# Start rows kept in registers, a region of rows per expert, a shorter plan and three smaller edits in a routed attention and expert kernel

## What is computed

```python
x = x + xattn(layernorm(x), ctx, ctx, mask, Wq, Wk, Wv, bq, bk, bv)   # relu(relu(q k^T)/sqrt(d) + mask) v), relu
h = layernorm(x)
topv, topi = top_k(h @ gate_w, 2);  w = softmax(topv)                  # 8 experts, 2 per token
Y[e] = (silu(h @ Wu[e]) * (h @ Wv[e])) @ Wo[e]
x = x + w[0] * Y[topi[0]] + w[1] * Y[topi[1]]
```

## Time and profile before

| | |
|---|---|
| median of 3 runs | 445.58 us (444.45 to 448.17) |
| profiled execution | 448.33 us, its span 446.6 us |
| busy: TensorE, its weight loads | 92%, 81% |
| busy: VectorE, ScalarE, GpSimd | 78%, 60%, 44% |
| mean granted TensorE clock | 0.982 |
| DMA moved | 97.99 MB, mean 219 GB/s |

### The profile page before, as it was taken

The page is one execution under the profiler, slowest core; times in us unless marked ns, Lnnn a source line. Parts: engine busy times, 40 slices in busy tenths (PEclk is TensorE's granted clock), DMA queues, the critical chain, the costliest instruction groups (busy, mean ns, idle before and its releaser), DMA issues.

```text
span 446.6 us, 10603 instructions
## 1 busy us (share of the span) xinstructions
PE 409.9 (92%) x3066; PEld 362.5 (81%) x3066; DVE 347.0 (78%) x1138; ACT 267.2 (60%) x581; POOL 195.3 (44%) x234
## 2 busy tenths in 40 slices
PE   8999999999999999989898999899999968979790
PEld 6688998888888998878787888799998857968670
DVE  2679899999999999998678888578877656657560
ACT  1677777787877778767575566576664423333230
POOL 2011245555555656653467432333331535554441
PEclk9999999999999999999999999999999999898995
DMA  8713234766666664535768699799746989898831
GB/s 294 236 61 96 94 115 173 280 237 221 236 240 240 239 231 167 181 133 176 262 199 274 234 288 295 238 316 288 228 102 185 322 271 296 273 299 284 280 143 47
DMA packets 53623, 97.99 MB, mean 219 GB/s; under 512 B 8384, under 2 KB 19136, under 8 KB 53440
## 3 DMA queue, kind: packets, MB, share of 16 engines
q1 hardware_dynamic: 41648, 63.21, 45.9%
q0 software_dynamic: 11920, 34.10, 20.2%
HBM read 54.15 MB, written 50.80 MB: 235 GB/s over the span
## 4 chain that ended last, share of the span: by engine, by line
PE 39%; DVE 22%; SPq 16%; issue 9%; ACT 6%; DMA 4%; POOL 1%; POOLq 0%; DVEq 0%; ACTq 0%
PE psQ L1513 6%; SPq L506 6%; PE psQ L1514 6%; PE psQ L1515 6%; DVE st L1122 4%; DVE x L1111 3%; PE psT L1509 3%; PE psS L1513 2%; DVE qpT L932 2%; SPq L521 2%; SPq L528 2%; DMA vp<-acc_dram 2%; PE psS L1515 2%; PE psS L1514 2%; SPq L535 1%
## 5 line engine op out<-in xcount | busy, mean ns | idle before, releaser
L932 DVE TENSOR_TENSOR qT<-psT,qT 128x512 fp32r<-128x512 f32 x103 | 69.3, 686 | 25.1 <-ACT qT L728 24.8
L1513 PE MATMUL psQ<-wuv,qT 128*128 x284 | 87.0, 306 | 0.0
L634 POOL DMA_INDIRECT z_dram<-zb x64 | 71.4, 1116 | 31.3 <-issue 15.2
L1514 PE MATMUL psQ<-wuv,qT 128*128 x284 | 81.1, 286 | 0.0
L1515 PE MATMUL psQ<-wuv,qT 128*128 x284 | 80.7, 284 | 0.0
L1513 PE MATMUL psQ<-qT,wq 128*128 128x256 f32 x256 | 75.2, 294 | 0.0
L1515 PE MATMUL psQ<-qT,wq 128*128 128x256 f32 x256 | 72.4, 283 | 0.0
L1514 PE MATMUL psQ<-qT,wq 128*128 128x256 f32 x256 | 72.4, 283 | 0.0
L728 ACT ACTIVATE qT<-psT 128x512 fp32r<-128x512 f32 x103 | 59.4, 594 | 17.4 <-PE psT L1509 17.4
L1513 PEld LDWEIGHTS psQ<-wuv,qT 128*128 128x128 f32 x284 | 54.2, 191 | 3.2 <-issue 0.2
L1515 PEld LDWEIGHTS psQ<-wuv,qT 128*128 128x128 f32 x284 | 54.7, 192 | 0.0
(11 more groups left out here) (333 smaller groups left out, 1074.2 us busy)
## 6 DMA issues: line engine op xcount, KB each, us to landing
wq<-z_dram SPq DMA_DIRECT2D x42, 264.0 KB, 3.7
xin<-in_x_dram SPq DMA_DIRECT2D x11, 512.0 KB, 3.7
z_dram<-spare SPq DMA_DIRECT2D x17, 264.0 KB, 3.8
qpT<-z_dram SPq DMA_DIRECT2D x17, 264.0 KB, 4.0
acc_dram<-spare SPq DMA_DIRECT2D x17, 256.0 KB, 3.9
xin<-acc_dram SPq DMA_DIRECT2D x16, 256.0 KB, 3.7
vp<-acc_dram SPq DMA_DIRECT2D x14, 256.0 KB, 3.8
kpT<-z_dram SPq DMA_DIRECT2D x10, 264.0 KB, 3.4
```

The source lines that it names most:

```text
L634: pool.indirect_dma_start(out=z_dram, out_offset=bass.IndirectOffsetOnAxis(ap=z_of(b)[:, t, ROW_COL + k:ROW_COL + k + 1].bitcast(U32), axi ...
L932: nc.vector.tensor_tensor(o, a, b, ALU.subtract).then_inc(s, 1)
L1513: pe.matmul(o, w[LO], a[HI], start=first, stop=False)
L1514: pe.matmul(o, w[HI], a[LO], start=False, stop=False)
```

## The change

- **Slots in registers.** SyncE reads the row of a tile from 39 on once, in `load_z`, and keeps it in a register for `load_acc`. The rows of the 14 held tiles are read two at a time ahead of tiles 43 to 49 (`know_held`). Before tile 50 five `load_acc` are issued instead of nine, and later ones follow the `z_dram` loads by four to six tiles instead of two; `load_held` stands behind `load_z` and `load_acc` of its tile instead of ahead.
- **Five places** for what is added to held tiles instead of three.
- **One region of 8192 rows per expert**: firsts from its bottom up, seconds from its top down (a sign is multiplied in where the place is written). The constant rows behind the seconds have fixed addresses and are stored in blocks 4 to 11; `fill_pad` (8 DMAs with a row read, tiles 17 to 24) is gone. `copy_tail` reads two rows instead of one.
- **A shorter plan.** The expert of a tile is its row shifted right by 13 bits. The chains have 10, 15 and 30 instructions instead of 13, 17 and 38, and are cut into tiles in another way; the third part is read out one tile later.
- **Scores wait by chunk**: each chunk waits for its own low half.
- **Logit strips turned plainly**: two 128x128 transposes, and VectorE adds the four strips (`folded`) ahead of the choice of experts.
- **x normalised on ScalarE**: both halves; VectorE's `norm_x` goes from the block.

```diff
 
-CAP = TOK + 2 * P
-DUMMY = K * E * CAP
-NROWS = DUMMY + P
+
+
+LOG_CAP = 13
+CAP = 1 << LOG_CAP
+TOP = TOK + 2 * P
+NROWS = E * CAP
+DUMMY = NROWS - P
...
-PLANNED = (13, 30, 68)
+CONSTS = 20
+
+PLANNED = (10, 25, 55)
 
 
 def ge(eng, sem, value):
...
-        extra = [vp_flat[:, i * D:(i + 1) * D] for i in range(3)]
+        extra = [vp_flat[:, i * D:(i + 1) * D] for i in range(4)] + [kpT_flat[:, 2 * ROW:2 * ROW + D]]
...
                 if 4 <= b.n < 4 + E:
-                    e = b.n - 4
-                    sp.dma_start(z_dram[K * e * CAP:K * e * CAP + P, :], spare[:, :]).then_inc(head_stored, 16)
-                    sp.dma_start(acc_dram[(K * e + 1) * CAP:(K * e + 1) * CAP + P, :], spare[:, 0:D]).then_inc(head_stored, 16)
+                    at = (b.n - 4) * CAP
+                    sp.dma_start(z_dram[at:at + P, :], spare[:, :]).then_inc(head_stored, 16)
+                    sp.dma_start(z_dram[at + TOP:at + TOP + P, :], spare[:, :]).then_inc(pad_stored, 16)
+                    sp.dma_start(acc_dram[at + TOP:at + TOP + P, :], spare[:, 0:D]).then_inc(acc_pad_stored, 16)
 
...
-                row = row_of(t)
-                sp.dma_start(zg_of(t), z_dram[bass.ds(row, P)]).then_inc(z_loaded[q], 16)
-
-            def load_acc(t, row):
+                rows[t] = row_of(t)
+                sp.dma_start(zg_of(t), z_dram[bass.ds(rows[t], P)]).then_inc(z_loaded[q], 16)
+                if t < FIRST_B:
+                    del rows[t]
+
+            def load_acc(t):
 
                 q, old = t % RING, t - RES_B
                 if old >= FIRST_B:
                     sp.wait_ge(res_stored[old % RING], 16 * (rounds(old) + 1))
-                sp.dma_start(res_of(t), acc_dram[bass.ds(row, P)]).then_inc(acc_loaded[q], 16)
+                sp.dma_start(res_of(t), acc_dram[bass.ds(rows[t], P)]).then_inc(acc_loaded[q], 16)
+                del rows[t]
 
             def load_held(h):
 
                 i = h % len(extra)
                 ge(sp, held_ready, h - len(extra) + 1)
+                sp.dma_start(extra[i], acc_dram[bass.ds(held_rows[h], P)]).then_inc(held_loaded[i], 16)
+                del held_rows[h]
+
+            def know_held(h):
                 sp.wait_ge(kinds, 3)
-                row = sp.value_load(held_row[0:1, h:h + 1], min_val=0, max_val=DUMMY)
-                sp.dma_start(extra[i], acc_dram[bass.ds(row, P)]).then_inc(held_loaded[i], 16)
...
+            def tail_row(k, e):
+                return sp.value_load(tail_i[0:1, k, e:e + 1], min_val=0, max_val=DUMMY - P)
 
             def copy_tail(e):
 
-                sp.wait_ge(pads_known, 2)
-                ge(sp, head_stored, 32 * E if e == 0 else 0)
-                row = sp.value_load(tail_i[0:1, e:e + 1], min_val=0, max_val=DUMMY - P)
-                sp.dma_start(z_dram[(K * e + 1) * CAP:(K * e + 1) * CAP + P, :], z_dram[bass.ds(row, P)]).then_inc(tail_copied, 16)
...
-
-            held_at = [FIRST_B + RING + 1 + 4 * h // 3 for h in range(HELD)]
...
+
...
+                sp.dma_start(acc_dram[bass.ds(tail_row(1, e), P)], spare[:, 0:D]).then_inc(acc_head_stored, 16)
+
+
+            bulk = FIRST_B + RING - 1
+            accs = {bulk - 1: [FIRST_B + LATE, FIRST_B, FIRST_B + 1, FIRST_B + LATE + 1, FIRST_B + LATE + 2]}
+            todo = list(range(FIRST_B + LATE + 3, TILES))
+            for t in range(bulk, TILES):
+                accs[t] = [todo.pop(0) for _ in range(2 if t in (bulk + 4, bulk + 6) else 1)]
+            accs[TILES] = todo
             for t in range(TILES):
                 if EARLY <= t < EARLY + E:
+                    if t == EARLY:
+                        sp.wait_ge(pads_known, 2)
+                        sp.wait_ge(head_stored, 16 * E)
                     copy_tail(t - EARLY)
-                    fill_pad(t - EARLY)
                 if FULL + 2 <= t < FULL + 2 + E:
-                    fill_acc_pad(t - FULL - 2)
-                if t == FIRST_B + RING - 1:
+                    fill_acc(t - FULL - 2)
+                if bulk - HELD // 2 <= t < bulk:
+                    for i in range(2):
+                        know_held(2 * (t - bulk + HELD // 2) + i)
+                if t == bulk:
                     sp.wait_ge(acc_pad_stored, 16 * E)
+                    sp.wait_ge(acc_head_stored, 16 * E)
                     sp.wait_ge(acc_spare_stored, 16)
-                    for a in range(FIRST_B - RING, FIRST_B - 1):
+                    for a in range(FIRST_B - RING, FIRST_B):
                         sp.wait_ge(res_stored[a % RING], 16 * (rounds(a) + 1))
-                    first = FIRST_B + LATE
-                    order = [first] + list(range(FIRST_B, first)) + list(range(first + 1, FIRST_B + RES_B))
-                    ahead = [row_of(a) for a in order[:LATE + 1]]
-                    sp.wait_ge(res_stored[(FIRST_B - 1) % RING], 16 * (rounds(FIRST_B - 1) + 1))
-                    for a, row in zip(order, ahead):
-                        load_acc(a, row)
-                    for a in order[LATE + 1:]:
...
-                        load_acc(a, row_of(a))
-                for h in range(HELD):
-                    if held_at[h] == t:
-                        load_held(h)
+                    for a in accs[t - 1]:
+                        load_acc(a)
                 load_z(t)
-                if t >= FIRST_B + RING - 1:
-                    load_acc(t - RING + 1 + RES_B, row_of(t - RING + 1 + RES_B))
-            for t in range(TILES - RING + 1 + RES_B, TILES):
-                load_acc(t, row_of(t))
+                if t >= bulk:
+                    for a in accs[t]:
+                        load_acc(a)
...
+                                     scale=rstd1[:, t:t + 1]).then_inc((xn0_ready, xn1_ready)[t], 1)
 
...
+                    norm1(nxt, 0)
                     norm1(nxt, 1)
...
+                    link(nc.vector.tensor_copy(length[:, :], len_i[:, :]))
                 else:
-                    link(nc.vector.tensor_copy(length[:, :], total[:, :]))
+                    link(nc.vector.tensor_tensor(length[:, :], len_i[:, :], used[:, :], ALU.subtract))
 
             def plan_ends(g):
...
+                if g == 1:
+                    link(nc.vector.tensor_tensor(jump[:, 0:1], jump[:, 0:1], used[:, 0:1], ALU.add))
                 link(nc.vector.tensor_reduce(red_f[:, :], jump[:, :], AX.X, ALU.add))
-
-            def plan_rows(g):
-
-                if g == 1:
-                    link(nc.vector.scalar_tensor_tensor(row_f[:, :], red_f[:, :], used[:, 0:1], tile_p[:, :], ALU.add, ALU.add))
-                else:
-                    link(nc.vector.tensor_tensor(row_f[:, :], red_f[:, :], tile_p[:, :], ALU.add))
-                link(nc.vector.tensor_scalar(exp_f[:, :], exp_f[:, :], float(E - 1), None, ALU.min))
...
-                nc.vector.tensor_copy(sched_row[:, first:end], bank[0:1, off:off + end - first]).then_inc(sched_ready, 1)
-                nc.vector.tensor_copy(sched_exp[:, first:end], bank[0:1, off + P:off + P + end - first]).then_inc(sched_ready, 1)
+                if g < 2:
+                    nc.vector.tensor_copy(sched_row[:, first:end], bank[0:1, off:off + end - first]).then_inc(sched_ready, 1)
+                else:
+                    nc.vector.tensor_scalar(sched_row[:, first:end], bank[0:1, off:off + end - first], float(DUMMY), None,
+                                            ALU.min).then_inc(sched_ready, 1)
+                dve.wait_ge(sched_ready, 2 * g + 1)
+                nc.vector.tensor_scalar(sched_exp[:, first:end], sched_row[:, first:end], LOG_CAP, None,
+                                        ALU.logical_shift_right).then_inc(sched_ready, 1)
 
...
+                    nc.vector.tensor_reduce(logits[:, :, :], ps_strips, AX.X, ALU.add).then_inc(folded, 1)
+                    ge(dve, folded, self.b.n + 1)
                     for t in range(TPB):
-                        nc.vector.max(top_v[:, t, :], ps_logit[:, t, :]).then_inc(route, 1)
+                        nc.vector.max(top_v[:, t, :], logits[:, t, :]).then_inc(route, 1)
...
-                    nc.vector.tensor_copy(z_of(self.b)[:, :, ROW_COL:ROW_COL + K].bitcast(U32), destf[:, :, :]).then_inc(place, 1)
+                    nc.vector.tensor_tensor(z_of(self.b)[:, :, ROW_COL:ROW_COL + K].bitcast(U32), destf[:, :, :], sign[:, :, :],
+                                            ALU.mult).then_inc(place, 1)
...
-                    norm_x(nxt)
                 if third.real:
...
                 if t == 13:
-                    lists_ends(range(0, 5))
+                    lists_ends(range(0, 3))
                 if t == 14:
+                    lists_ends(range(3, 5))
                     lists_starts()
                 if t == 15:
                     lists_skips()
                 if t == 16:
                     lists_rows()
                 if t == 17:
+                    lists_heads()
+                if t == 18:
                     lists_cuts()
-                if t == 19:
+                if t == 20:
```

(7 more changed lines are left out.)

118 lines of the change are left out of this document (56 added, 62 removed).

## The result

The changed kernel takes **430.96 us** (median of four, 428.88 to 431.29) against 446.23 us before (median of four, run beside it): a ratio of **0.9647, 95% interval 0.9595 to 0.9699**. The forecast was 421 us, in a range of 411 to 433. The gain is real and its main cause is as forecast, but the estimate is 10 us too low. Ratios here use only executions within 1.5% of the fastest of the same kernel, medians use all.

What follows compares the result with a forecast made beforehand. The prediction took SyncE's own instructions to bound the last 29 tiles. Blocks -4.3 - 0.3, tiles 7 to 24 -4.5 and tiles 41 to 70 -15 - 0.5 made -24.6, so 445.6 - 24.6 = 421 us, range 411 to 433.

Steps and rivals of the forecast that it cites:

- What bounds the kernel: Last 29 tiles: SyncE's own instructions, row reads included, hold them back, losing 19.2 us against TensorE's floor of 2.67 each.
- Registers and order: Tiles 41 to 70: fewer row reads on SyncE and a new load order give -15, `acc_dram` loads of tiles 43 and 44 -0.5 us.
- shares of 1.0 and 0.91: Tiles 41 to 70: full DMA share would give -16 us, the sustained 0.91 only -8; -15 was taken.
- Regions and plan: Tiles 7 to 24: no `fill_pad` and a shorter plan give -4.5 us, bounds -1 and -6.5.
- The plan's part: Tiles 7 to 17: fewer linked VectorE instructions, 0.20 us a link, give -1.5 us.
- The block: Attention blocks: next queries 0.33 us sooner in each of 13 blocks, -4.3 us; strips, fold and links before the last expert load, -0.3.
- (1) DMA binds harder: Last tiles: DMA share stays at 0.91 or stores land later, final stage -8, 428 to 433 us; chance 0.17.
- (2) The floor everywhere: TensorE's floor holds in the last 29 tiles, -19, with full gains elsewhere, 412 us; chance 0.14.
- (3): Another wait, VectorE or GpSimd's stores, takes SyncE's place; gain under 1%, 441 to 450 us; chance 0.05.
- (4): Last 29 tiles slower: early loads crowd out stores they wait for, landings of 11 us, some 452 us; chance 0.04.
- (5) Slow stores into regions 16 MiB apart: Tiles 0 to 38: stores into the `acc_dram` regions at half speed cost about 8 us, 429 us; chance 0.03.
- The base: Whole kernel: all terms, -24.6 us, taken off the median of 445.6, 2.75 us below the profiled execution.

Runs made afterwards that it cites:

- e7_nine_ahead: Changed kernel with nine `acc_dram` loads issued ahead of tile 50 and none between tiles 46 and 50: 429.03 us, ratio 0.9606 to before.
- e3_chunk_alone: Kernel before with one edit, each product of the scores waiting for its own chunk of the low half: 460.45 us, ratio 0.9954 to before.
- e5_reread: Changed kernel with SyncE reading the row number again for every `acc_dram` and held load: 447.09 us, ratio 1.0012 to before.

## Why the prediction was right or wrong

**What bounds the kernel: right.** SyncE's own instructions held back the last 29 tiles. Putting the reads back undoes the whole change, and taking out those of `load_acc` alone gives 11.7 of some 15 us.

**Registers and order, -15 and -0.5: right in mechanism, 1.5 us too much.** The choice between shares of 1.0 and 0.91 came out above both for 45 us (1.04) and below both over the 65 us of the earlier trace rows (0.88): the loads were done sooner. What kept the stage from the floor was not DMA's total work, as the term assumed, but two covers at its start that were too short. The prediction gave the later `acc_dram` loads "5 and more" tiles until they are used; that of tile 46, queued behind `z_dram` loads which waited for the stores of tiles 39 and 40, went out at 347.81 and was used at 353.50, 2.1 tiles later. It gave the held loads "over 2" tiles, 5.3 us; the one that held back tile 50 was wanted 4.25 us after its issue (VectorE waited 1.5 us for it) and took 5.78 to land. The two tiles lost 3.6 us together; `e7_nine_ahead`, which moves the `acc_dram` loads, won back 1.15 of the first and nothing of the second. The reads moved ahead of tiles 43 to 49 cost nothing: tiles 43 to 47 took 2.67 to 2.68 each.

**Regions and plan, -4.5: -3.0.** The rounds of SyncE fell from 4.20 to (275.27 - 251.49) / 7 = 3.40 us, better than the 3.7 forecast, and tiles 17 to 24 gained 2.4 (19.9 against 22.3); the load of tile 25 then waited 1.94 us for the last `copy_tail` (1.2 was allowed for it). The plan's part is what failed: -1.5 was set for tiles 7 to 17, and they gave +0.2 (tiles 7 to 12) and -0.8 (12 to 17). Fewer links at 0.20 us each were counted, but tiles 8 and 10 still take 4.7 and 3.9 us. What holds these two was not tried. The eight constant stores added to the blocks were hidden, as said: a share of 0.67 for 0.62, the same period.

**The block, -4.3 and -0.3: this step failed,** measured -0.7 in all. The prediction let ScalarE's normalisation start "at 153.08 as before", added up one block's rows from there, and read the 0.33 us by which the next queries came out sooner as a gain in the period. That the rows agree to 0.05 us is luck: the block as a whole lay 0.28 us sooner in the span, ScalarE started 0.30 us later in it than before, and the next queries not sooner at all. A period shortens only if every closed chain does, and ScalarE's start was the end of one on which the prediction had put nothing: GpSimd's `rstd`, which follows its scatters, which follow VectorE's last low half. In the old kernel that chain was 11.70 us long (`e3_chunk_alone`), so no gain on TensorE could have given more than 0.14 us a block; in the new one it is 11.80, by longer instructions on GpSimd. And with GpSimd out of the way TensorE's row is 11.64, 0.2 below before, where 0.38 to 0.57 was claimed. The signal that the prediction named for this failure, blocks of 11.8 with ScalarE ahead of the third group, is what the profile shows.

**Rivals.** (1) DMA binds harder: not on the chip of the result; on the two slower ones it is not shown, since DMA's share in the last stage was lower there (0.78). (2) The floor everywhere: no, though DMA allowed it for 45 us (the rate it needs is 26.8 MB in 77 us, 348 GB/s, and not 335). (3), (4): no; the landing of a `vp` load went from a median of 3.6 us to 6.0 over 355 to 400 us, not to 11. (5) Slow stores into regions 16 MiB apart: none. From 215 GB/s at a share of 0.62 to 234 at 0.67, bytes per share stay the same, 347 and 349 GB/s.

**The base.** 2.75 us of the miss is that the terms came from a profiled execution longer than its median, and were taken off the median whole. Which stage of that execution was the longer one can't be said: there is no second trace of before.

## What to carry to other kernels

When a queue's instructions have no gap between them, count the instructions per unit of work: taking a register read out of each load was worth more than the deeper buffers and the better order together. A gain inside a loop body counts only if it is on every closed chain of the loop; follow the chain of waits around one whole period, GpSimd included, before adding up positions, and count positions from the start of the body and not from that of the span. And the same change can be worth 15 us on one chip and 8 on another: measure before and after on the same chip, and on a second one.

## What the runs showed of the hardware

**Chips of one kind can differ by more than the change is worth.** The same code took 431 and 454 us. The blocks (DMA share 0.67) were alike to 0.1 us, the last stage was not (82.6 against 98.8 us). The traces of the slower chips have waits without a cause in the program (the page's "another core or an unknown queue" has 5% of after's chain there; on the other chip it is absent). The Trainium skill, "DMA: Bandwidth & Descriptors", Bandwidth, says that when both cores on one memory stream, each gets about half of its bandwidth, some 358 GB/s, and that its higher figures are for a core whose partner is idle. The 376 GB/s held for 45 us in the trace of after agree with an idle partner. A busy one might be behind the slower chips, but no run here shows who else used the memory, and it stays open.

**A row read has no fixed price.** Of the 53 reads of L521 in `e5_reread`'s last stage the shortest took 263 ns, the median one 273 and the longest 1089. Why some take four times as long the runs don't tell.
